# A three-layer cross network on one core: the first layer repacked into six full tiles and a rest of 12 pairs, the last layer's end moved one chunk later, and another order of the start

## The reference

```python
x0 = xk = inputs                                   # (512, 39, 16), float32
for idx, (W, b) in enumerate(params):
    z = relu(einsum('bhd,bkd,hks->bsd', x0, xk, W) + b[None, :, None])
    if idx != 2:
        xk = z[:, :64, :]                          # input maps of the next layer
        direct.append(z[:, 64:, :])
    else:
        direct.append(z)
logit = sum over d of concatenate(direct, axis=1)  # (512, 256)
```

## Time and profile before

| quantity | value |
| --- | --- |
| time, median of 3 runs | 577.89 us (576.62 to 577.9) |
| time of the profiled execution | 578.04 us |
| span of that execution in the trace | 576.2 us |
| PE / DVE / POOL / ACT busy, share of the span | 96% / 95% / 85% / 67% |
| mean granted TensorE clock | 0.993 of full |

### The profile page before, as it was taken

How to read it: one execution, slowest core, us unless ns; L and a number is a source line. 1 busy time by engine, 2 the same in 40 slices (tenths; PEclk the granted TensorE clock), 3 DMA queues, 4 the chain that set the end, 5 groups by cost and what they waited for, 6 DMA issues and landing times.

```text
span 576.2 us, 6174 instructions
## 1 busy us (share of the span) xinstructions
PE 555.9 (96%) x2040; PEld 384.9 (67%) x2040; DVE 544.6 (95%) x501; ACT 386.1 (67%) x417; POOL 492.3 (85%) x212
## 2 busy tenths in 40 slices
PE   3789999999999999999999999999999999999997
PEld 1355767767766776776767676776776677677664
DVE  2689999999999999999999999999999999999985
ACT  0556777676776767668576767757677676766673
POOL 0575979989797997979799797988979799797986
PEclk9799999999999999999999999999999999999999
DMA  8986848092763909357291844819275390923300
GB/s 245 420 322 227 357 150 361 17 379 115 268 244 108 399 3 367 144 218 294 68 380 63 328 183 173 338 28 400 82 287 225 125 387 1 389 121 127 110 2 19
DMA packets 20828, 122.09 MB, mean 212 GB/s; under 512 B 2686, under 2 KB 3644, under 8 KB 10556
## 3 DMA queue, kind: packets, MB, share of 16 engines
q1 hardware_dynamic: 20652, 121.70, 54.5%
q10 hardware_dynamic: 144, 0.00, 0.0%
HBM read 121.16 MB, written 0.52 MB: 211 GB/s over the span
## 4 chain that ended last, share of the span: by engine, by line
PE 89%; DMA 3%; DVE 3%; issue 2%; ACT 2%; SPq 1%; DVEq 0%; ACTq 0%
PE z L467 89%; DMA spread<-x_spread 3%; DVE raw L313 1%; ACT hi L508 1%; DVE d_raw L313 1%; ACT w_hi L514 1%; DVE w_hi L351 0%; DVE exact L313 0%; SPq L243 0%; SPq L217 0%; SPq L242 0%; SPq L229 0%; SPq L237 0%; ACT maps L524 0%; ACT z L541 0%
## 5 line engine op out<-in xcount | busy, mean ns | idle before, releaser
L404 POOL TENSOR_TENSOR lo<-raw,hi 128x1024 fp32r<-128x1024 f32 (+1 forms) x206 | 488.6, 2408 | 62.3 <-ACT hi L508 62.3
L508 ACT ACTIVATE hi<-raw 128x1024 fp32r<-128x1024 f32 (+1 forms) x206 | 218.5, 1061 | 117.2 <-DVE raw L313 108.5
L313 DVE TENSOR_TENSOR raw<-spread,maps 128x1024 f32<-128x1024 f32 x191 | 227.9, 1214 | 13.1 <-ACT maps L524 12.6
L467 PE MATMUL z<-hi,w_hi 128*128 128x512 f32 (+1 forms) x568 | 226.6, 399 | 7.0 <-ACT hi L508 5.1
L467 PE MATMUL z<-hi,w_lo 128*128 128x512 f32 (+1 forms) x536 | 212.7, 397 | 0.0
L467 PE MATMUL z<-lo,w_hi 128*128 128x512 f32 (+1 forms) x568 | 208.3, 461 | 0.0
L467 PE MATMUL z<-exact,w_exact 128*128 128x512 f32 (+2 forms) x368 | 177.9, 604 | 10.0 <-DVE exact L313 10.0
L467 PEld LDWEIGHTS z<-lo,w_hi 128*128 128x128 f32 (+1 forms) x568 | 106.8, 188 | 62.9 <-issue 42.1
L467 PEld LDWEIGHTS z<-hi,w_hi 128*128 128x128 f32 (+1 forms) x568 | 107.0, 188 | 36.9 <-issue 7.7
L467 PEld LDWEIGHTS z<-hi,w_lo 128*128 128x128 f32 (+1 forms) x536 | 101.1, 189 | 24.3 <-issue 0.2
L467 PEld LDWEIGHTS z<-exact,w_exact 128*128 128x128 f32 (+2 forms) x368 | 70.7, 193 | 63.5 <-issue 43.5
(11 more groups left out here) (15 smaller groups left out, 50.0 us busy)
## 6 DMA issues: line engine op xcount, KB each, us to landing
spread<-x_spread SPq DMA_DIRECT2D x80, 1024.0 KB, 7.0
fields<-x_fields SPq DMA_DIRECT2D x32, 768.0 KB, 6.8
fields<-x_fields SPq DMA_DIRECT2D x16, 512.0 KB, 5.6
spread<-w1s SPq DMA_DIRECT2D x2, 512.0 KB, 13.1
spread<-w2s SPq DMA_DIRECT2D x2, 512.0 KB, 5.0
w_exact<-w2e SPq DMA_DIRECT2D x1, 512.0 KB, 17.8
out<-sums SPq DMA_DIRECT2D x2, 240.0 KB, 3.6
w_exact<-w1e SPq DMA_DIRECT2D x1, 256.0 KB, 10.1
```

What stands on the lines that cost most here:

```text
L313: nc.vector.tensor_tensor(products, by_field, by[0:rows, :].unsqueeze(1).to_broadcast([rows, tiles, COLS]), ALU.mult).then_inc(ready, 1)
L404: nc.gpsimd.tensor_tensor(lo[0:rows, count % LO_RING, :, :], raw[0:rows, PLACE[S][layer, c, k] % RAW_RING, :, :], hi[0:rows, count % HI_RI ...
L467: mm = nc.tensor.matmul(z_of(layer, c)[:, :], w[0:rows, :], part[0:rows, :], start=(couples[0] == 0 and step == 0 and p == 0), stop=(coupl ...
L508: nc.scalar.activation(hi[0:rows, count % HI_RING, :, :], products, ACT.Copy).then_inc(hi_ready, 1)
```

## The change

It has four parts.

1. Layer 0's 780 pairs are placed freely on the partitions: six tiles of 128 rows (768 pairs) and a seventh with the 12 pairs that are left. The products of those 12 stand three times in that tile, at partitions 0, 32 and 64 (76 rows in all, the ones between unused). This tile is of kind S. ACT rounds all 76 rows; POOL then overwrites the first 12 of `hi` with the rest; the tile's rounded weights stand at rows 0 and 32, the weights' rest at row 64. One matmul of 76 rows does all three products. The hi step of this couple is skipped.
2. The couples 7 to 9 of layer 2 of chunk c run after layer 1 of chunk c+1, in every chunk (before, only in the last). The lo steps come one couple behind in layers 1 and 2, two in layer 0, and run on over the border of a segment. The kinds are in another order, as many of each in layers 1 and 2. Rings: `exact` 4, `raw` 6, `hi` 5, `lo` 4. Layer 2's output goes to an SBUF tile (`final`) before it is summed, and `direct` has two halves. ACT evacuates chunk c's layer 1 at another place.
3. Chunk 0 is nearly all E: EEEE in layer 0, nine of ten couples in layer 1, seven of ten in layer 2. The weights of layers 1 and 2 are loaded whole, in five parts, into their own tiles; ACT and POOL split them part by part.
4. Layer 0 of chunk 1 starts early: its first two couples, of kind E, run right behind layer 0 of chunk 0, from fields loaded into two slots of `spread`; its couples are E, E, E and the rest. Three matmuls on zeros run on PE before anything else.

```diff
-KINDS = ("SDEE", "SSEDSSSEDS", "SDSSSEESDS")
-KINDS_FIRST = ("EEEE", "SSEDSSSEDS", "ESESSEESDS")
+KINDS = ("SDES", "ESDSESSDSS", "SSDSSESDES")
+KINDS_FIRST = ("EEEE", "ESEEEEEEEE", "EESEEESEES")
+EARLY = 2
+KINDS_SECOND = E * EARLY + KINDS[0][EARLY:]
-LO_LAG = 2
-D_LAG = 2
-EXACT_RING = 3
-RAW_RING = 3
-HI_RING = 6
-LO_RING = 5
+LO_LAGS = (2, 1, 1)
+D_LAG = 3
+EXACT_RING = 4
+RAW_RING = 6
+HI_RING = 5
+LO_RING = 4
 def segments():
     yield 0, 0, range(COUPLES[0])
-    for c in range(LAST):
+    yield 0, 1, range(EARLY)
+    for c in range(CHUNKS):
         yield 1, c, range(COUPLES[1])
-        yield 0, c + 1, range(COUPLES[0])
-        yield 2, c, range(KEPT if c == LAST - 1 else COUPLES[2])
-    yield 1, LAST, range(COUPLES[1])
-    yield 2, LAST - 1, range(KEPT, COUPLES[2])
-    yield 2, LAST, range(COUPLES[2])
+        if c:
+            yield 2, c - 1, range(KEPT, COUPLES[2])
+        if c < LAST:
+            yield 0, c + 1, range(0 if c else EARLY, COUPLES[0])
+        yield 2, c, range(KEPT if c < LAST else COUPLES[2])
...
+            load_fields(0, 0)
+            sp.dma_start(w0_staged[:, W0_CUTS[1]:, :, :], w0[:, W0_CUTS[1]:, :, :]).then_inc(w0_loaded[1], 16)
+            load_fields(0, 1)
+            load_fields(0, 2)
+            load_early(0)
+            load_early(1)
+            for q in range(QUADS):
+                load_weights(1, q)
+                load_spread(0, q)
             load_fields(1, 0)
-            load_spread(0, 3)
-            load_fields(1, 1)
-            load_spread(0, 4)
             load_fields(1, 2)
-            sp.dma_start(w_exact[2][:, :, :], w2e).then_inc(w_exact_loaded[2], 16)
-            load_weights(2, 0, w2s)
-            load_weights(2, 1, w2s)
+            for p in range(QUADS):
+                load_weights(2, p)
...
+            def weights_last_split_lo(n):
                 last = len(SPLIT_TILES[n]) - 1
-                dve.wait_ge(weights_hi[n], parts)
-                nc.vector.tensor_tensor(w_lo[n][:, a:last, :], w_staged[n][:, a:last, :],
-                                        w_hi[n][:, a:last, :].bitcast(fp32), ALU.subtract).then_inc(weights_lo[n], 1)
-                nc.vector.tensor_tensor(w_hi[n][HALF:128, last, :], w_staged[n][HALF:128, last, :],
+                dve.wait_ge(weights_hi[n], len(RUNS[n]))
+                nc.vector.tensor_tensor(w_hi[n][HALF:128, last, :], w_exact[n][HALF:128, TILES - 1, :],
                                         w_hi[n][HALF:128, last, :].bitcast(fp32),
-                                        ALU.subtract).then_inc(weights_lo[n], 1)
+                                        ALU.subtract).then_inc(weights_last_lo[n], 1)
...
+                    if what == "hi" and rest(layer, k):
+                        continue
...
+                        if rest(layer, k):
+                            rows = REST if what == "exact" else ROWS_REST
+                            low = high
...
+            pe.wait_ge(warm_ready, 1)
+            for _ in range(WARM):
+                nc.tensor.matmul(z[2][:, :], final[:, 0:OUT], final[:, :], start=True, stop=True)
             contract(0, 0, range(COUPLES[0]))
+            contract(0, 1, range(EARLY))
...
                 else:
                     split_hi(1, c, range(0, COPY_AT))
-                    copy_fields(c + 1)
-                    split_hi(1, c, range(COPY_AT, FINISH_AT))
+                    if c < LAST:
+                        copy_fields(c + 1)
+                    split_hi(1, c, range(COPY_AT, COUPLES[1]))
...
+                    split_hi(2, c - 1, range(KEPT, COUPLES[2]))
+                if c < LAST:
+                    split_hi(0, c + 1, range(0, MAPS2_AT) if c else range(EARLY, COUPLES[0]))
+                spread_maps2(c)
+                if 0 < c < LAST:
+                    split_hi(0, c + 1, range(MAPS2_AT, COUPLES[0]))
+                split_hi(2, c, range(0, FINISH_AT))
+                if c:
                     finish_last(c - 1)
-                    split_hi(1, c, range(FINISH_AT, COUPLES[1]))
-                split_hi(0, c + 1, range(COUPLES[0]))
...
+                split_hi(2, c, range(FINISH_AT, MAPS1_AT))
+                if c < LAST:
+                    spread_maps1(c + 1)
+                split_hi(2, c, range(MAPS1_AT, KEPT if c < LAST else COUPLES[2]))
             finish_last(LAST)
```

More of the change, by code:

```diff
@@ new lines, with schedules @@
+SEGMENTS = list(segments())
+def schedules():
+    at, pending = 0, []
+    for layer, c, couples in SEGMENTS:
+        todo = []
+        for k in couples:
+            kind = kinds(layer, c)[k]
+            todo.append(("exact" if kind == E else "hi", layer, c, k))
+            if kind != E:
+                pending.append((at + LO_LAGS[layer], layer, c, k))
+            for p in sorted(pending):
+                if p[0] <= at and k != couples[-1]:
+                    pending.remove(p)
+                    todo.append(("lo",) + p[1:])
+            at += 1
+        ends = layer == 1 or (layer, c) == (2, LAST)
+        for p in sorted(pending):
+            if p[0] < at or ends and (p[1] == 1 or c == LAST):
+                pending.remove(p)
+                todo.append(("lo",) + p[1:])
+        yield todo
@@ new lines, with runs_of @@
+SCHEDULES = list(schedules())
+FIRST_STEP, LAST_STEP = {}, {}
+for _step in sum(SCHEDULES, []):
+    FIRST_STEP.setdefault(_step[1:3], _step)
+    LAST_STEP[_step[1:3]] = _step
+def runs_of(n):
+    runs = []
+    for p, first in enumerate(WEIGHT_CUTS[:-1]):
+        for t in [t for t in SPLIT_TILES[n] if first <= t < WEIGHT_CUTS[p + 1]]:
+            if runs and runs[-1][0] == p and runs[-1][2] == t:
+                runs[-1][2] = t + 1
+            else:
+                runs.append([p, t, t + 1])
+    return runs
@@ L91 @@
+RUNS = [None, runs_of(1), runs_of(2)]
 PLACE = {E: {}, S: {}, D: {}, "SD": {}}
-for _layer, _c, _couples in segments():
+for _layer, _c, _couples in SEGMENTS:
     for _k in _couples:
         _kind = kinds(_layer, _c)[_k]
[L95 to L110, removed]
@@ L113, in cin_kernel @@
-def cin_kernel(nc, x_fields, x_spread, w0, w0t, w1e, w1s, w2e, w2s, b, out):
+        for _ring in PLACE:
+            if _kind in _ring:
+                PLACE[_ring][_layer, _c, _k] = len(PLACE[_ring])
+COUPLE = {ring: list(places) for ring, places in PLACE.items()}
+LOW = [_step[1:] for _step in sum(SCHEDULES, []) if _step[0] == "lo"]
+USED = {couple: n for n, couple in enumerate(LOW)}
+S_LOW = {couple: n for n, couple in enumerate(c for c in LOW if c in PLACE[S])}
+assert len(USED) == len(PLACE["SD"])
@@ L114, in cin_kernel @@
+def cin_kernel(nc, x_fields, x_spread, w0, w1, w2, b, out):
     fp32 = mybir.dt.float32
@@ L192, in wait_contracted @@
         def wait_contracted(engine, layer, c):
-            what, k = schedule(layer, c, [k for n, m, ks in segments() if (n, m) == (layer, c) for k in ks])[-1]
+            what, _, _, k = LAST_STEP[layer, c]
             if what == "exact":
@@ L427, in contract @@
             def contract(layer, c, couples):
-                order = schedule(layer, c, couples)
-                tiles = LAYER_TILES[layer]
-                for step, (what, k) in enumerate(order):
+                for step in SCHEDULES[SEGMENTS.index((layer, c, couples))]:
+                    what, layer, c, k = step
+                    if what == "hi" and rest(layer, k):
+                        continue
+                    tiles = LAYER_TILES[layer]
                     kind = kinds(layer, c)[k]
@@ L508, in split_hi @@
-                    nc.scalar.activation(hi[0:rows, count % HI_RING, :, :], products,
-                                         ACT.Copy).then_inc(hi_ready, 1)
-            def weights_split_hi(n, h):
-                a, e = halves(n)[h]
-                act.wait_ge(w_split_loaded[n][h], 16)
-                nc.scalar.activation(w_hi[n][:, a:e, :], w_staged[n][:, a:e, :],
-                                     ACT.Copy).then_inc(weights_hi[n], 1)
+                    rows, tiles = ROWS_REST if rest(layer, k) else 128, tiles_in(layer, k)
@@ new lines, in split_hi, with weights_split_hi @@
+                    products = raw[0:rows, place % RAW_RING, 0:tiles, :] if kind == S else d_raw[0:rows, 0:tiles, :]
+                    nc.scalar.activation(hi[0:rows, count % HI_RING, 0:tiles, :], products,
+                                         ACT.Copy).then_inc(hi_ready, 1)
+            def weights_split_hi(n, t):
+                for p, a, e in RUNS[n]:
+                    if a == t:
+                        m = SPLIT_TILES[n].index(a)
+                        act.wait_ge(w_loaded[n][p], 16)
+                        nc.scalar.activation(w_hi[n][:, m:m + e - a, :], w_exact[n][:, a:e, :],
+                                             ACT.Copy).then_inc(weights_hi[n], 1)
```

464 lines of the change are left out of this document (253 added, 211 removed).

## The result

The changed kernel takes 562.69 us (median of 4 runs, 562.27 to 563.09) against 577.89 (4 runs, 576.62 to 578.42): a ratio of 0.9737, 95% interval 0.9726 to 0.9749. The forecast was 565.0 with a range of 560 to 573; the gain is 15.2 us where 12.9 were forecast. The profiled execution took 562.33 us with a span of 560.5 us.

A forecast was written before the change was run, and what follows sets the result against it. PE was taken as the bound at 33.53 us a chunk: 53.6 start + 503.0 for 15 chunks + 0.3 + 0.8 + 1.0 + 1.4 + 3.2 = 563.3 us span, stated as 565.0 us with time around it; range 560 to 573.

The forecast's parts named there:

- PE sets a period: Regular chunks: PE's passes and records set the pace, 34.15 us before and 33.53 after the change.
- 0.05 us a chunk: Regular chunks: charge for what the hand-made layout misses, 15 x 0.05 = 0.8 us in all.
- 33.5 from the count and 33.59 from the rows: DVE's list in a regular chunk: 33.5 us by counting instructions, 33.59 us by a cross-check on profile rows.
- the 8.7 us that the passes promised: Layer 0's seventh tile as one pass: PE's period 0.62 us shorter in each of 14 chunks.
- an engine misfit: Rival: in each chunk PE waits for a lo step, 0.4 us a chunk, 570.5 us; chance 22%.
- POOL as the bound: Rival: POOL keeps its 3.2 us idle a chunk, period 35.3 us, end 592; chance 9%.
- The start: Chunk 0: DVE's first layer 1 product at 22.3 us, layer 2 at 42.45, chunk 1's layer 1 on PE at 53.6.
- the rate of the first 14 us of loads: Start: loads move at 245 GB/s over the first 14.4 us, so chunk 0's last fields land at 14.95 us.
- the range's lower end: Down to 560 us, if the early loads are faster than the 245 GB/s of before.
- the warm-up matmuls, put at nothing in the sum: Start: three matmuls on zeros should help PE's clock, but layer 0 was taken to end at 18.8 us either way.
- The slow subtraction: Early chunks' 64 x 128 weight subtraction on DVE, both operands in SBUF: stall between 0.3 and 2.34 us, taken as 1.0.
- The end: Last chunk: POOL's last lo steps come 1.4 us after PE asks, charged at 1.4 us.

The follow-up runs named there:

- e1: Changed kernel with one hi pass with the weights' rest (layer 1, tile 5) left out in chunks 1 to 15, shortening PE's list; 562.42 us.
- e3: Changed kernel without that hi pass and with DVE's second reduction summing one of 32 examples in chunks 0 to 14; 558.69 us.
- e4: Changed kernel with layer 0's rest tile contracted exactly (2 records of 12 rows instead of one 76-row pass); 575.46 us, ratio 0.996.
- e5: Changed kernel with layer 2's couples 7 to 9 put back into their own chunk, in all chunks; 586.24 us, ratio 1.0132.
- e8: Changed kernel without the three matmuls on zeros at the start; 563.81 us, ratio 0.9745.
- e11: Changed kernel with the two subtractions on 64 x 128 weights of layers 1 and 2 moved from DVE to POOL; 561.31 us, ratio 0.9710.

## Why the prediction was right

**The pace.** The step that failed is "PE sets a period": the sum gave PE's 33.53 us and charged 0.05 us a chunk for what the layout missed. The period is 33.58, but it is DVE's own list (28 x 1.13 and the rest, plus the 0.1 us that `d_raw` costs), as e1 to e3 show. The prediction had both numbers for DVE, 33.5 from the count and 33.59 from the rows, and went by the count. That the period came out to the hundredth is luck: the two lists are 0.05 apart, and the 0.05 a chunk was charged for gaps that a layout by hand misses, not for DVE. e4 shows that the tile's kind is what brings the period below 34.15: the 8.7 us that the passes promised, less 0.7 for DVE.

**The fit of the engines.** DVE no longer waits for maps, POOL idles 1.5 us a chunk (1.19 in front of the 12-row step, 0.15 behind it and 0.17 once more) where 1.3 were laid out, its 12-row subtraction takes 1.28 where 1.31 were taken from a row with 117 rows. The rivals of an engine misfit and of POOL as the bound did not come; with layer 2's end put back (e5) a slower kernel than before is what one gets, through ACT's `final` and not through POOL's idle time; how much of that is the place of ACT's step stays open.

**The start.** Each step was laid out right and came 2.5 to 2.9 us sooner: layer 1 of chunk 0 at 19.36 where 22.3 was written, layer 2 at 39.89 for 42.45, chunk 1 at 51.10 for 53.6. The term that was mis-sized is the rate of the first 14 us of loads, taken from the old order at 245 GB/s and measured at 326; it was kept for the range's lower end. DVE waits for chunk 0's last fields up to 11.03 us, where 14.95 was written. But the loads alone don't give the 2.5 us: the warm-up matmuls, put at nothing in the sum because the fields were to come at 14.95 anyway, are needed too. Without them (e8) layer 1 starts at 21.25 and chunk 1 at 52.99, only 1.05 and 0.6 us sooner than written; the other 1.9 us come with them. Both together are nearly the whole difference between 563.3 and the span of 560.5. Why the new order loads faster no run shows.

**The slow subtraction.** Taken at 1.0 us between 0.3 and 2.34: it took 1.83 and 0.30 ahead of it, and moving it gave 0.9 to 1.5 us (e11). With both operands in SBUF it took 1.83 us beside a running POOL instruction. Its 12-row sister shows the cause: in the changed kernel it starts at 33.44, beside no POOL instruction, and takes 0.28; in e11 the same instruction starts at 32.50, 0.23 us after the start of a POOL subtraction that takes 1.26, and takes 1.18 itself. By the Trainium skill (SBUF — State Buffer, Who interferes with whom) a DVE instruction with two SBUF inputs and a GpSimd instruction that reads SBUF exclude each other for a whole instruction; the rows agree.

**The end.** Chunk 9 starts layer 1 on PE at 320.68 and the last matmul ends at 557.26: less six periods, 35.1 us are left for the last chunk, 1.6 more than PE's list, where 1.4 were charged. From 51.10 to 320.68 are eight periods and 0.9 us, 0.3 of it the two E couples that were counted.

## What to carry to other kernels

When a change brings two engines' lists within a tenth of a microsecond, shortening either alone is worthless: shorten each, and then both, to see which sets the pace. An engine's own list must include its waits on its own single buffers: where a count and a stretch of rows differ, the rows have them in. Where a kernel's first work is moved, look at what else was done ahead of it at no cost, such as ACT's table load, and take the rate of the first loads as open.

## What the runs showed that I had not expected

In these runs a matmul with few rows is not cheaper, and an exact one can cost more. Tiles of 117, 78 and 76 rows fit the price of a full one, but the exact 12-row tile of e4 makes its own weight loads and the next ones late, 0.40 us in all. In the changed kernel the 64-row tile at the end of chunk 0's layer 1 shows the same gap (0.76 us ahead of its loads and 0.76 behind, where 0.24 is usual):

```profile
35.10 0.19 PEld L611 LDWEIGHTS z<-exact,w_exact 128*128 128x128 f32 x1 [0.24 <-issue]
36.05 0.29 PEld L611 LDWEIGHTS z<-exact,w_exact 64*128 64x128 f32 x2 [0.76 <-issue]
37.10 0.30 PEld L611 LDWEIGHTS z<-exact,w_exact 128*128 128x128 f32 x2 [0.76 <-issue]
37.64 0.19 PEld L611 LDWEIGHTS z<-exact,w_exact 128*128 128x128 f32 x1 [0.24 <-issue]
```

Five loads at the usual 0.43 us would take 2.14 us, and from 35.10 to 37.64 are 2.54: again 0.40 us. The 12-row tile of chunk 0's layer 0, which is exact too, has the same two gaps (loads at 14.22 and 15.27 us). Whether chunk 0 would gain these 0.40 us with 128 rows there (the second half with zero weights) was not tried.
